# Last stage of a four-block attention program: transposes issued ahead of the projection g of x, and the last tile's copy of transposed probabilities made in halves

## The reference

```python
B, C, CI, T = (8, 64, 32, 256)
g_x = jnp.einsum('oc,bct->bto', Wg, x_this) + bg
theta = jnp.einsum('oc,bct->bot', Wtheta, x_this) + btheta[None, :, None]
phi = jnp.einsum('oc,bct->bot', Wphi, x_other) + bphi[None, :, None]
f = jnp.einsum('bci,bcj->bij', phi, theta)
f_div_C = jax.nn.softmax(f, axis=-1)
y = jnp.einsum('bij,bjo->bio', f_div_C, g_x)
w_y = jnp.einsum('oc,btc->bot', Wz, y) + bz[None, :, None]
mean = jnp.mean(w_y, axis=(0, 2), keepdims=True)
var = jnp.var(w_y, axis=(0, 2), keepdims=True)
w_y = gamma[None, :, None] * (w_y - mean) * jax.lax.rsqrt(var + EPS) + beta[None, :, None]
return w_y + x_this
```

## Time and profile before

| | us |
|---|---|
| median of 3 runs | 1640.72 |
| lowest and highest | 1638.94, 1641.45 |
| the profiled execution's own time | 1641.74 |
| its span in the trace | 1640.1 |
| PE busy in the span | 1565.3 (95%) |
| last stage: first transpose (tile 0) to the DVE add of the last w_y | 1555.86 to 1626.31 |

### The profile page before, as it was taken

One profiled execution on the slowest core, in us unless ns is written; L12 is line 12 of the kernel. 1 busy time (PEld: TensorE's weight loads), 2 busy tenths in 40 slices (PEclk: granted clock), 3 DMA queues, 4 the chain that ended last, 5 costly groups with the idle time before them and its releaser, 6 DMA issues. The chain is left out here.

```text
span 1640.1 us, 47131 instructions
## 1 busy us (share of the span) xinstructions
PE 1565.3 (95%) x20204; PEld 1384.8 (84%) x20204; DVE 1001.5 (61%) x2047; ACT 855.8 (52%) x1595; POOL 299.5 (18%) x317
## 2 busy tenths in 40 slices
PE   8999999999999999999999999999989989889995
PEld 6988988888888888888889889888878888879863
DVE  7755555555686555555556664688876568865366
ACT  5544444444454444444444565667665556555575
POOL 1211101101222110111011130401203130201042
PEclk9999999999999999999999999999999999999998
DMA  5100000001000100100000000300001010000001
GB/s 200 34 34 34 2 34 34 34 2 34 34 1 34 34 34 2 34 34 2 33 28 27 2 27 1 105 3 3 2 28 53 1 45 13 3 2 27 14 14 52
DMA packets 18717, 46.40 MB, mean 28 GB/s; under 512 B 1456, under 2 KB 11712, under 8 KB 15440
## 3 DMA queue, kind: packets, MB, share of 16 engines
q1 hardware_dynamic: 14320, 39.17, 7.0%
q10 hardware_dynamic: 4192, 4.24, 0.8%
HBM read 39.21 MB, written 4.19 MB: 26 GB/s over the span
## 5 line engine op out<-in xcount | busy, mean ns | idle before, releaser
L175 PE MATMUL ps<-ch,W 128*128 128x512 f32 (+1 forms) x2592 | 603.9, 380 | 5.4 <-DVE W L243 2.5
L175 PEld LDWEIGHTS ps<-ch,W 128*128 128x128 f32 x2592 | 444.4, 190 | 87.5 <-issue 4.4
L175 PEld LDWEIGHTS ps<-W,split_arena 128*128 128x128 f32 x3084 | 395.9, 190 | 39.3 <-issue 12.2
L175 PE MATMUL ps<-W,split_arena 128*128 128x256 f32 x3084 | 411.8, 285 | 17.5 <-DVE split_arena L1011 10.2
L175 PE MATMUL ps<-W,ch 128*128 128x256 f32 x1632 | 223.4, 286 | 0.0
L175 PEld LDWEIGHTS ps<-W,ch 128*128 128x128 f32 x1632 | 203.5, 190 | 0.3 <-ACT arena L740 0.2
L706 ACT ACTIVATE arena<-ps 64x256 f32<-64x256 f32 x256 | 97.2, 380 | 193.1 <-PE ps L619 190.0
L797 DVE TENSOR_REDUCE small<-ps 128x4 f32<-128x260 f32 x128 | 54.3, 424 | 204.0 <-PE ps L581 204.0
L755 ACT ACTIVATE arena<-ps,hbias 128x512 f32<-128x512 f32 x128 | 88.2, 689 | 126.4 <-PE ps L175 126.4
L880 DVE TENSOR_TENSOR arena<-ps,arena 128x512 f32<-128x512 f32 x128 | 88.0, 692 | 106.8 <-PE ps L175 105.6
L1011 DVE TENSOR_TENSOR split_arena<-arena,split_arena 128x512 fp32r<-128x512 f32 x96 | 70.1, 730 | 126.0 <-ACT split_arena L1043 119.7
(11 more groups left out here) (134 smaller groups left out, 1964.2 us busy)
## 6 DMA issues: line engine op xcount, KB each, us to landing
raw<-wpack SPq DMA_DIRECT2D x23, 1028.0 KB, 4.9
arena<-vb_in SPq DMA_DIRECT2D x16, 256.0 KB, 5.1
x_sb<-x_in SPq DMA_DIRECT2D x4, 512.0 KB, 8.4
arena<-ctxT SPq DMA_DIRECT2D x4, 512.0 KB, 9.1
spill<-x_sb ACTq DMA_DIRECT2D x1, 2048.0 KB, 9.0
arena<-spill ACTq DMA_DIRECT2D x1, 2048.0 KB, 9.0
arena<-ctx_tok SPq DMA_DIRECT2D x16, 128.0 KB, 2.1
out<-x_sb SPq DMA_DIRECT2D x7, 256.0 KB, 2.5
```

What stands on the lines that cost most here:

```text
L175: last = e.matmul(dst, lhs[a], rhs[b], start=start and n == 0, stop=stop and n == 2, skip_group_check=True)
```

## The change

It does two things, in the last stage only.

1. In pe_tiles the call of pe_turn(t-1) moves from the end of a step to the place in front of pe_gx(t) and pe_wy(t-2).
2. For the last tile alone (u == LAST) the transposes signal after each bank, ACT copies fT in two halves of 512 columns instead of one of 1024, and pe_y waits for each half in front of the matmuls that need it. To allow that, pe_y's two loops change places for all tiles: the head a is now outside, jh inside.

```diff
@@ pe_turn
-            ins.then_inc(zT_done, 1)
+                if a == 1 or u == LAST:
+                    ins.then_inc(zT_done, 1)
@@ pe_y
-            e.wait_ge(fT_ok, u + 1)
             e.wait_ge(gx_ok, min(u + 2, TILES))
-            for jh in range(2):
-                for a in range(2):
+            for a in range(2):
+                e.wait_ge(fT_ok, u + 1 + (a if u == LAST else 0))
+                for jh in range(2):
@@ pe_tiles
+                if 1 <= t <= TILES:
+                    pe_turn(e, t - 1)
                 if t < TILES:
                     pe_gx(e, t)
                 if t >= 2:
                     pe_wy(e, t - 2)
-                if 1 <= t <= TILES:
-                    pe_turn(e, t - 1)
@@ act_tiles
-                    e.activation(cut(fT, 2), ps[:, BZ[0]:BZ[0] + 2, :], ACT.Copy).then_inc(fT_ok, 1)
+                    if u < LAST:
+                        e.activation(cut(fT, 2), ps[:, BZ[0]:BZ[0] + 2, :], ACT.Copy).then_inc(fT_ok, 1)
+                    else:
+                        for a in range(2):
+                            e.wait_ge(zT_done, u + 1 + a)
+                            e.activation(fT[:, a * 2 * D:(a + 1) * 2 * D], ps[:, BZ[a], :], ACT.Copy).then_inc(fT_ok, 1)
```

## The result

The changed kernel takes 1649.08 us (median of 5 runs, 1647.35 to 1649.59), the kernel before 1641.18 us (median of 5, 1638.94 to 1645.57). The ratio is 1.0044, with a 95% interval from 1.0028 to 1.0060: slower by 7.9 us in the medians, clear of noise. The profiled execution took 1649.08 us with a span of 1647.5 us.

The account below looks back on a forecast made before the run. A circle from PE's transposes through g of x, Wz, DVE's add and reciprocal and POOL was to take 5.29 us per tile against 4.50; -0.1 + 10.3 - 0.3 = +9.9 us, median 1640.72 to 1650.6, range 1647.5 to 1653.5.

Parts of the forecast that it names:

- The reading of the chain: PE, last stage: g of x, behind the transposes, waits for yT, 0.50 us idle; 0.29 us per tile to be had.
- The second circle: Last stage: transposes, g of x, Wz product, DVE's add and reciprocal, POOL, back to transposes; closes within one tile, 5.29 us.
- the seven links: The waits and operations from one tile's transposes to the next, each read to about 0.02 us, in sum 5.29 us.
- The last link: From the end of POOL's multiply to the start of PE's transposes, 0.14 us, read at tile 0.
- The period: Time from transposes to transposes in the last stage: 5.29 us against 4.50, over 13 periods +10.3 us.
- The first step: From the first transposes, 1555.86, to the second, predicted at 1560.0 where they started at 1560.16: -0.1 us.
- The end: From tile 14's transposes to DVE's last add: 7.55 us where it was 7.87, -0.3 us (-0.2 to -0.5).
- The clock: Rival: PE's idle drops the clock to 1.2 GHz; 1681 us if for good, 1661 for a third of the stage; chance 0.03.
- main case: The slower kernel, paced by 5.29 us per tile in the last stage: 1648 to 1653 us, chance 0.86.
- The stretch that I leaned on: Trace of the kernel before: PE busy 2.21 of 4 us, clock at 1.00; the new order has PE busy four fifths.
- The values' swapped waits: The values' edit in pe_y, an extra semaphore and swapped loops: waits for nothing on the other 15 tiles, costs nothing.
- The rival on the other side: Reciprocal does not in effect wait behind the w_y add; PE sets the pace, 4.21 us per tile, 1636.2 us; chance 0.06.

Follow-up runs that it names:

- experiment with swapped waits: The kernel before with only the two waits in front of the values swapped, gx_ok first, then fT_ok: 1642.48 us, ratio 1.0011.
- kernel with filled idle: The changed kernel with four more unused matmuls in each even step where PE waits 1.46 us for POOL: 1648.72 us, ratio 1.0046.
- the two kernels with the 1.46 us idles: The changed kernel, 1649.08 us, and the changed kernel without the halves, only the transposes moved ahead of g of x, 1650.28 us.

## Why the prediction was right, point by point

**The reading of the chain** held: the place of the transposes was the only cost on PE's side, 0.50 us of idle, and it went away. **The second circle** closed as worked out, with POOL releasing the transposes in all 14 steps, odd and even alike. Its length was 5.06 and not 5.29 us, and three of the seven links were mis-sized:

| link | predicted | measured |
|---|---|---|
| transposes to g of x | 0.97 | 0.93 |
| g of x to the product | 0.49 | 0.39 |
| product to bias, bias to reciprocal | 0.69, 0.86 | 0.69, 0.86 |
| reciprocal to POOL, POOL | 0.24, 1.90 | 0.24, 1.90 |
| POOL to transposes | 0.14 | 0.05 |

The last link came from the only row in which POOL had released PE, tile 0's. There POOL's semaphore is the last of two waits in pe_turn, behind the one for the block before; on all later tiles it is the first, ahead of fT_ok. The experiment with swapped waits measures this very difference at the values, 0.14 against 0.04 us; that it is the cause at the transposes too is argued from the code, not tested. The 0.49 us between g of x and the product was read where g of x had either waited for yT or followed other work; behind the transposes it was 0.39. I have no run that says why. Thirteen times 0.23 us is 3.0 us too much. The sum is off by only 2.8 us, 10.3 predicted and 7.5 measured, since it also took 4.50 us for each of the 13 steps before, 58.5 us, where they took 58.28 (seven of the thirteen are the short ones). The period is the term that was mis-sized, and the claim that it is good to 0.15 us was too narrow.

**The first step** came out at -0.40 for a predicted -0.1. There is no w_y bias in it yet: its links are 0.90 to g of x, 0.60 from there to its bias, for which the prediction took the product's 0.69, 0.20 to the reciprocal, 0.25 to POOL, 1.90, and 0.05 from POOL to PE, in sum 3.90 us. **The end** was to be 7.55 us (-0.3). With the clock at full level it is 7.64 us (1623.87 to 1631.51 in the kernel with filled idle), -0.23; the copies of 512 columns took 0.594 us on average for an assumed 0.60. In the changed kernel's own trace it was 8.91 us, because the clock fell there. **The clock** I gave 0.03, as a fall for good or for a third of the stage. What happened lies between that rival and none: two short falls, 1.56 us and about 1.3 us. The prediction had named a clock below 1.00 in the stage as a sign that it is wrong; that sign appeared, and its main case, with no fall at all, is not what the traces show. The stretch that I leaned on, PE busy 2.21 of 4 us at clock 1.00, did not exclude it. The Trainium skill (TensorE: Matmul & The Clock Gate, section A second HAM failure mode) says that short idles between groups of matmuls can make the clock alternate; the traces of the two kernels with the 1.46 us idles agree, with two falls each. The price was 2.8 us in the changed kernel, not the 10 to 30 us of the prediction's rival.

So the number came out right partly by luck: 2.8 us less from the circle and 0.3 less from the first step, against 2.8 more from the clock and 0.1 more at the end, make a stage of +9.73 for a predicted +9.9. Without the clock's falls the same way of adding gives +6.9 and 1647.6 us, at the very lower edge of the range. The medians say +7.9, inside the range, 1649.08 for 1650.6, with an interval of 4.6 to 9.8 us that just takes in the stage's +9.73. **The values' swapped waits**, costed at nothing, are indeed hidden in the changed kernel, as the values are in no circle there; in the old order they would have cost 1.3 us. **The rival on the other side**, a gain to 1636.2 us, decides where the reciprocal does not stand behind the w_y bias. Made so, it gave 1635.2. Its price had been nearly right, its condition not met.

## What to carry to other kernels

When an instruction with a late wait is moved ahead on an in-order engine, look at what now stands behind it, and follow those results until they come back to what the wait is for. If they do, through any engine's list, the sum of that circle is the new step time, and today's chain of waits does not show it; it shows only as slack. Then the other engine's list has to change together with the move: here one move in DVE's list turned +0.44% into -0.34%, and alone the move on PE gave a loss of 0.57% and the move on DVE nothing.

## What the runs showed of the hardware that was not expected

- Of two waits in front of one PE instruction, the order matters. With the late semaphore written first PE starts 0.04 us after the release, with the late one last 0.14 us, and where the wait lies in a circle this came back in every step: 1.34 us in 16 tiles (stage 70.45 to 71.79 us). Shown at the values; only argued at the transposes.
- The granted clock fell to its lower level of 1.2 GHz in a stage with an idle of 1.46 us in every second step, after PE had been busy 15.20 of 20 us:

```profile
1604.70:1624.70 20.00, 15.20 (x128) 9.89 (x126) 11.39 (x27) 12.68 (x41) 7.57 (x4) 1.00 0.00 1
```

  It fell twice in each of the two traces with that idle; each fall in the changed kernel cost 1.3 to 1.6 us. In the one trace with matmuls without use in that idle it did not fall, and the stage was shorter by 2.7 us.
